# Row maxima of the second attention turned by VectorE in 32x32 blocks instead of by TensorE, and each unit's sums copied before a step's first exponential

## What is computed

```python
qkv = x @ w_qkv                      # x: layer norm of the tokens, (4, 1024, 256)
q, k, v = ...                        # 8 heads of 32 channels
dots = jnp.einsum('bhid,bhjd->bhij', q, k) * scale
attn = jax.nn.softmax(dots, axis=-1)
out = jnp.einsum('bhij,bhjd->bhid', attn, v)
t = t + out @ w_out + b_out
```

## Time and profile before

| | |
|---|---|
| time, median of 3 runs | 1183.61 us (1182.93 to 1188.93) |
| span of the profiled execution | 1183.2 us |
| busy, share of the span | PE 93%, PEld 62%, DVE 69%, ACT 53%, POOL 51% |
| mean granted TensorE clock | 0.985 of full |
| units whose row is turned in the second attention | 31 (one more is turned before it) |
| costliest groups beside PE's | L953 ACT 268.6 us, L1739 DVE 287.0 us, L699 POOL 197.8 us |

### The profile page before, as it was taken

The page is one execution under the profiler, slowest core; times in us unless marked ns, Lnnn a source line. Parts: engine busy times, 40 slices in busy tenths (PEclk is TensorE's granted clock), DMA queues, the critical chain, the costliest instruction groups (busy, mean ns, idle before and its releaser), DMA issues.

```text
span 1183.2 us, 28483 instructions
## 1 busy us (share of the span) xinstructions
PE 1105.0 (93%) x10344; PEld 728.7 (62%) x10344; DVE 818.8 (69%) x1493; ACT 628.7 (53%) x1144; POOL 600.2 (51%) x513
## 2 busy tenths in 40 slices
PE   7999999978999999999999989898999999999995
PEld 4454645434444454555445545687899988989883
DVE  4666566766788788788878892768555656655773
ACT  3566676546677666766775665453333333333332
POOL 3424242314888763775477546167545445544540
PEclk9999999989999999999999999999999999999999
DMA  5356842626123230433243213723333233323328
GB/s 173 89 181 211 311 160 94 184 69 196 51 56 87 82 82 29 104 100 98 68 115 91 60 43 100 303 38 77 53 54 54 43 52 55 46 46 47 46 38 289
DMA packets 98884, 120.60 MB, mean 102 GB/s; under 512 B 29024, under 2 KB 76064, under 8 KB 98112
## 3 DMA queue, kind: packets, MB, share of 16 engines
q1 hardware_dynamic: 75280, 70.40, 20.3%
q0 software_dynamic: 20400, 42.08, 15.9%
q10 hardware_dynamic: 3072, 6.30, 1.5%
HBM read 73.10 MB, written 45.47 MB: 100 GB/s over the span
## 4 chain that ended last, share of the span: by engine, by line
PE 70%; DVE 11%; issue 6%; DMA 6%; ACT 3%; DVEq 3%; POOL 1%; SPq 1%; ACTq 0%; POOLq 0%
PE PP L1023 21%; PE PP L1448 11%; PE PP L1307 9%; PE PP L1333 8%; PE PP L1122 3%; DVE mxp L1739 3%; PE PP L1254 3%; PE PP L1194 3%; PE PP L1039 3%; PE PP L1322 2%; PE PP L1317 2%; DMA res_d<-WORK,lb 2%; PE PP L1154 1%; DVEq L2016 1%; DVE WORK L2017 1%
## 5 line engine op out<-in xcount | busy, mean ns | idle before, releaser
L953 ACT ACTIVATE WB<-PP 128x512 f32<-128x512 f32 x512 | 268.6, 606 | 146.1 <-PE PP L1333 146.0
L1739 DVE TENSOR_REDUCE mxp<-PP 128x2 f32<-128x1024 f32 x242 | 287.0, 1219 | 62.3 <-PE PP L1254 62.0
L993 ACT ACTIVATE WORK<-PP,b1c 128x256 f32<-128x256 f32 (+1 forms) x320 | 139.4, 450 | 239.4 <-PE PP L1023 191.7
L699 POOL TENSOR_TENSOR WB<-WB 128x1024 f32<-128x1024 f32 x84 | 197.8, 2358 | 89.4 <-PE PP L1322 58.7
L782 POOL DMA_INDIRECT res_d<-WORK,lb x70 | 117.6, 1680 | 157.8 <-DVE WORK L2034 144.7
L1448 PE MATMUL PP<-WB,WORK 128*128 x1704 | 193.8, 274 | 0.0
L1023 PE MATMUL PP<-WORK,WB 128*128 128x256 f16 (+1 forms) x1552 | 175.9, 273 | 2.4 <-DVE WORK L2003 1.7
L1448 PEld LDWEIGHTS PP<-WB,WORK 128*128 128x128 f16 x1704 | 165.2, 98 | 19.6
L1023 PE MATMUL PP<-WORK 128*128 128x128 f16 (+6 forms) x1086 | 161.1, 300 | 11.3 <-DVE WORK L1656 3.6
L1023 PEld LDWEIGHTS PP<-WORK,WB 128*128 (+1 forms) x1552 | 152.2, 102 | 22.2 <-issue 4.8
L1333 PE MATMUL PP<-WORK 97*128 97x256 f16 x1024 | 158.0, 277 | 6.7 <-ACT WB L953 4.2
(11 more groups left out here) (319 smaller groups left out, 1205.1 us busy)
## 6 DMA issues: line engine op xcount, KB each, us to landing
WORK<-in_L_ffn_W_dram POOLq DMA_DIRECT2D x32, 512.0 KB, 4.3
res_d<-WORK SPq DMA_DIRECT2D x8, 1024.0 KB, 5.2
late_d<-WB POOLq DMA_DIRECT2D x1, 6144.0 KB, 19.3
WB<-late_d ACTq DMA_DIRECT2D x3, 2048.0 KB, 14.0
v_d<-WORK SPq DMA_DIRECT2D x4, 1024.0 KB, 5.2
WORK<-q_hi_d SPq DMA_DIRECT2D x16, 256.0 KB, 3.7
WORK<-v_d SPq DMA_DIRECT2D x8, 512.0 KB, 5.6
WORK<-k_hi_d SPq DMA_DIRECT2D x16, 256.0 KB, 3.9
```

The source lines that it names most:

```text
L699: pool.tensor_tensor(PS[n % 2], PR[n % 3][:, 0], PR[n % 3][:, 1], ALU.add).then_inc(s("pair_kept"), 1)
L953: act.activation(PR[n % 3][:, c // 2, c % 2 * 2:c % 2 * 2 + 2], SCORES[m % 3] .rearrange("p (h n) -> p h n", h=2), ACT.Exp).then_inc(s("e_ ...
L993: act.activation(hid[:, k, 0:width], hidden_bank(k)[:, 0:width], ACT.Gelu, bias=b1c[:, bass.ds(e, 1), k], scale=1.0 / WSCALE)\
L1739: dve.tensor_reduce(mxp[:, n // 4 % 2, i, h:h + 2, k], PP[2 + h // 2][:, :].rearrange("p (h n) -> p h n", h=2), X_AXIS, ALU.max).then_inc( ...
```

## The change

1. The row of maxima is turned by DVE. `turn_row` scales `mx` into a new SBUF tile `nm16` (128 x 2 x 32 in fp16, of which 2 x 4 are used), waits for that, and transposes 32x32 blocks into `nmr`, now 128 x 32 x 2. PE's transpose and DVE's copy out of PSUM are gone, and with them a slot in each unit.
2. A 32x32 transpose leaves 32 queries in a partition's row, so the row is stored with four DMAs of 4 x 64 values (one for each block of 32 partitions) instead of two of 4 x 128. For this the two query blocks of a unit are interleaved: the matmuls of maxima take every second query of 256 as weights (`max_queries`) instead of 128 in a row.
3. `keep_sums` stands ahead of a step's first exponential instead of behind it.
4. Of the last batch's tokens, the first unit's row is turned directly behind its joining, and PE's transpose and wait there are gone.

Line numbers in the diff's surroundings shift: `turn_row` is at L1614 to L1623 of the changed kernel.

```diff
@@ def group_place(n)
-    return unit // 4 % 2, unit % 4 * QN + i * P, k
+    return unit // 4 % 2, unit % 4 * QN, i, k
@@ buffers
-        nmr = sb("nmr", [2 * GH, P], F16)
+        nm16 = sb("nm16", [P, 2, D], F16)
+        nmr = sb("nmr", [P, D, 2], F16)
@@ SP: def store_max(b, u)
                 sp.wait_ge(s("nmr_kept"), b * UNITS + (u + 1))
                 par, at = u // 4 % 2, u % 4 * QN
-                for i in range(2):
-                    sp.dma_start(QP[QK_ROWS:QK_ROWS + 1, par, :, at + i * P:at + (i + 1) * P],
-                                 nmr[i * GH:(i + 1) * GH, :]).then_inc(s("ld_nm"), 16)
+                for q in range(P // D):
+                    sp.dma_start(QP[QK_ROWS:QK_ROWS + 1, par, :, at + 2 * D * q:at + 2 * D * (q + 1)],
+                                 nmr[q * D:q * D + GH, :, :]).then_inc(s("ld_nm"), 16)
@@ ACT: def attend(b)
                 for t in range(STEPS):
                     n = b * STEPS + t
+                    if t % 4 == 2 and n >= 6:
+                        keep_sums((n - 6) // 4)
                     if n >= 3:
                         act.wait_ge(s("pv_made"), FREE + n - 2)
                     for c in range(4):
...
-                        if c == 0 and t % 4 == 2 and n >= 6:
-                            keep_sums((n - 6) // 4)
@@ PE: maxima
+            def max_queries(rows_at, g, at, i):
+
+                return QM[rows_at, g, at + i:at + QN:2]
...
-                    mm = pe.matmul(PP[2 + h // 2][:, h % 2 * HALF:(h % 2 + 1) * HALF], QM[rows_at, g, at:at + P],
+                    mm = pe.matmul(PP[2 + h // 2][:, h % 2 * HALF:(h % 2 + 1) * HALF], max_queries(rows_at, g, at, i),
...
-            def max_row(b, u, before):
-
-                bank = next_slot(b, before)
-                pe.wait_ge(s("nm_kept"), b * UNITS + (u + 1))
-                pe.transpose(bank[0:2 * GH, 0:P], mx[:, :], identf[:, :]).then_inc(s("c_made"), 1)
@@ PE: def attend(b)
-                    u = row_unit(t, first, last)
-                    if u is not None:
-                        max_row(b, u, before)
@@ PE: tokens of the last batch
-                    pe.wait_ge(s("nm_kept"), 1)
...
-                    pe.transpose(PP[2][0:2 * GH, 0:P], mx[:, :], identf[:, :]).then_inc(s("c_made"), 1)
@@ DVE
+            def turn_row(b, u):
+
+                n = b * UNITS + u
+                dve.wait_ge(s("nm_kept"), n + 1)
+                dve.tensor_scalar(nm16[:, :, 0:GH], mx[:, :].rearrange("p (i h) -> p i h", i=2), 1.0 / MSCALE, None,
+                                  ALU.mult).then_inc(s("ns_kept"), 1)
+                dve.wait_ge(s("ns_kept"), n + 1)
+                if n:
+                    dve.wait_ge(s("ld_nm"), LOAD_ROW * n)
+                dve.transpose(nmr[:, :, :].rearrange("p c i -> p i c"), nm16[:, :, :]).then_inc(s("nmr_kept"), 1)
...
-            def keep_row(b, u, before):
-
-                bank = bank_made(before)
-                if b * UNITS + u > 0:
-                    dve.wait_ge(s("ld_nm"), 32 * (b * UNITS + u))
-                dve.tensor_scalar(nmr[:, :], bank[0:2 * GH, 0:P], 1.0 / MSCALE, None, ALU.mult)\
-                   .then_inc(s("c_kept"), 1)
...
                     u = row_unit(t, first, last)
                     if u is not None:
-                        keep_row(b, u, before)
-                        row_at = slots[0]
+                        turn_row(b, u)
```

More of the change, by code:

```diff
@@ L44 @@
 LOAD_MAX = 16 * 2
+LOAD_ROW = 16 * (P // D)
 QN = 256
@@ L75 @@
 NORM_PAIRS = {2: (0,), 3: (1, 2), 4: (3,)}
-BATCH_SLOTS = UNITS + NT + 1
-FIRST_SLOTS = 1 + UNITS
+BATCH_SLOTS = NT + 1
+COUNT_SLOTS = 1
 ROW = 2 * C
@@ L335, in slots_before @@
         def slots_before(b, first):
-            return FIRST_SLOTS - UNITS if first else b * BATCH_SLOTS + (FIRST_SLOTS - BATCH_SLOTS)
-        FINAL_SLOTS = FIRST_SLOTS + (B - 1) * BATCH_SLOTS
+            return 0 if first else (b - 1) * BATCH_SLOTS
+        FINAL_SLOTS = (B - 1) * BATCH_SLOTS + COUNT_SLOTS
         def slot_bank(before, k):
-            odd = before % 2 if isinstance(before, int) else FIRST_SLOTS % 2
-            return PP[2][:, (odd + k) % 2 * HALF:((odd + k) % 2 + 1) * HALF]
+            half = (before + k) % 2
+            return PP[2][:, half * HALF:(half + 1) * HALF]
         def hidden_bank(k):
@@ L1239, in next_slot @@
                 pe.wait_ge(s("mx_kept"), b * (2 * STEPS) + (2 * group[0] + 1))
-                if not isinstance(before, int) or before + at > others:
+                if before + at > others:
                     pe.wait_ge(s("c_kept"), before + (at - others))
@@ L1249, in max_group @@
                 pe.wait_ge(s("mx_kept"), b * (2 * STEPS) + 2 * n)
-                if not isinstance(before, int) or before + slots[0] > 0:
+                if before + slots[0] > 0:
                     pe.wait_ge(s("c_kept"), before + slots[0])
@@ L1524, in _ @@
             dve.memset(held16[:, :], 0.0)
+            dve.memset(nm16[:, :, :], 0.0)
             for i, dst in enumerate((wqT, wvT)):
@@ L1612, in keep_k, with join_halves @@
                                   kb.unsqueeze(1).broadcast_to((P, NT, P)), ALU.add).then_inc(s("k_kept"), 1)
+            def join_halves(u, b):
+                dve.wait_ge(s("mx_kept"), b * 2 * STEPS + 8 * (u + 1))
+                dve.tensor_reduce(mx[:, :], mxp[:, u % 2].rearrange("p i h k -> p (i h) k"), X_AXIS, ALU.max,
+                                  negate=True).then_inc(s("nm_kept"), 1)
+            def turn_row(b, u):
[7 more added lines that the diff above has]
+                dve.transpose(nmr[:, :, :].rearrange("p c i -> p i c"), nm16[:, :, :]).then_inc(s("nmr_kept"), 1)
             def early_max(j):
@@ L1650, in tokens @@
                     dve.drain()
-                    dve.tensor_reduce(mx[:, :], mxp[:, 0].rearrange("p i h k -> p (i h) k"), X_AXIS, ALU.max,
-                                      negate=True).then_inc(s("nm_kept"), 1)
+                    join_halves(0, 0)
+                    turn_row(0, 0)
                 dve.wait_ge(s("av_made"), b * NT + NT)
@@ L1673, in tokens @@
                 deviations("stat_kept")
-                if last:
-                    dve.wait_ge(s("c_made"), 1)
-                    dve.tensor_scalar(nmr[:, :], PP[2][0:2 * GH, 0:P], 1.0 / MSCALE, None, ALU.mult)\
-                       .then_inc(s("c_kept"), 1)
-                    dve.drain()
-                    dve.sem_inc(s("nmr_kept"), 1)
                 dve.wait_ge(s("sd_kept"), b + 1)
@@ L1740, in reduce_heads @@
                                   X_AXIS, ALU.max).then_inc(s("mx_kept"), 1)
-            def join_halves(u, b):
-                dve.wait_ge(s("mx_kept"), b * 2 * STEPS + 8 * (u + 1))
-                dve.tensor_reduce(mx[:, :], mxp[:, u % 2].rearrange("p i h k -> p (i h) k"), X_AXIS, ALU.max,
-                                  negate=True).then_inc(s("nm_kept"), 1)
-            def keep_row(b, u, before):
-                bank = bank_made(before)
-                if b * UNITS + u > 0:
-                    dve.wait_ge(s("ld_nm"), 32 * (b * UNITS + u))
-                dve.tensor_scalar(nmr[:, :], bank[0:2 * GH, 0:P], 1.0 / MSCALE, None, ALU.mult)\
-                   .then_inc(s("c_kept"), 1)
-            def row_kept(before, at):
-                dve.wait_ge(s("c_kept"), before + at)
-                dve.sem_inc(s("nmr_kept"), 1)
             logit, oh1, oh2, val, rest, tmp = [rt[:, i] for i in range(6)]
@@ L1941, in attend @@
                 slots[0] = 0
-                row_at = None
                 def tail_part(at):
@@ L1963, in attend @@
                     groups = max_groups(t, first, last)
-                    if row_at is not None:
-                        row_kept(before, row_at)
-                        row_at = None
                     joined = t + LEAD - 1
```

16 lines of the change are left out of this document (7 added, 9 removed).

## The result

| | before | changed |
|---|---|---|
| time, median | 1184.05 us (4 runs, 1182.93 to 1188.93) | 1204.18 us (4 runs, 1197.15 to 1210.04) |
| ratio to before, 95% interval | | 1.0158, 1.0107 to 1.0208 |
| span of the profiled execution | 1183.2 us | 1194.9 us (its own time: 1197.15 us, the lowest of the four) |
| mean granted TensorE clock | 0.985 | 0.981 |

The kernel became slower, by 20.1 us between the medians and by 18.7 us by the ratio. The prediction was 1201.2 us.

What follows compares the result with a forecast made beforehand. PE was taken to set the pace, with DVE free only about 0.55 us a step. The span of 1183.2 plus 23.3 for holds minus 5.7 of gains gave 1200.8, with 0.4 for the median 1201.2 us; range 1190 to 1211.

Steps and rivals of the forecast that it cites:

- The hold: DVE's new scaling between SBUF tiles (L1618) comes 0.4 us after POOL's addition L699 starts and stands until that ends.
- Its price: Delay per held unit: 1.49 us in the first batch (next maxima at 5.30 instead of 3.81), 1.0 us beside a projection.
- The count: Held: 7 first-batch units, t = 29 of second and third batch, t = 1, 5, 9 of three batches; 23.3 us.
- SP: SP's queue: four row DMA issues take about 2.5 us; row and sums just fit, by 0.3 us, and cost nothing.
- The gains: PE's transpose gone 3.3 us (30 by 0.11), copy ahead 1.9 (21 by 0.09), a slot less 0.5; together 5.7 us.
- Slow weights with a step of two: Rival: strided weight loads of the maxima cost 121 x 0.1 = 12 us on top of the hold: 1213; chance 0.03.
- Not held: Rival: the scaling L1618 isn't held by POOL, costs 0.2 us and fits the window: 1177.9 us; chance 0.12.
- nothing moves: Rival: holds cost half, POOL starting later relative to DVE, and the gains of 5.7 us cancel it: 1181 to 1187; chance 0.04.
- The margins give: Rival: row or sums land late, or the transpose is held or takes 0.55 us: about 1207 us; chance 0.08.

## Why the prediction was right, and where it was off

The time (1204.18 against 1201.2), the direction and the main mechanism held. Step by step:

- **The hold.** Right in place and kind. The scaling came 0.58 to 0.63 us into the step and stood until POOL's addition ended, 2.0 to 2.06 us. Shown by the reduction in its place (0.15 us, steps back to 2.90) and by the scaling added to the kernel before. The old scaling, which read PSUM, stood beside the same additions of POOL and was never held (source view, kernel before):

```profile
L1753 DVE TENSOR_SCALAR nmr<-PP x31: 267/269/279, 297.5 to 713.9; 8x128 f16<-8x128 f32 x31
```

- **Its price.** 1.31 us a unit in the first batch for 1.49. The group of maxima comes at 5.21 and not 5.30, mostly since the reductions start 0.08 us before the transpose's row ends; without a hold it would come at 3.85 and not 3.81, as the step before takes 3.09 and not 3.05; and PE wins 0.05 back behind it. Beside a projection 0.94 for 1.0.
- **The count.** 16 units, not 18. For t = 29 of the second and third batch I had read POOL's additions against a DVE that comes 0.6 us into the step. It comes 0.15 in, while POOL works at an L714 with an addition directly behind it. The timeline of DVE and POOL there, changed kernel:

```profile
514.62 1.15 POOL L714 TENSOR_TENSOR WORK<-WB,WORK 128x512 f16<-128x512 f32 x1
515.74 2.36 POOL L701 TENSOR_TENSOR WB<-WB 128x1024 f32<-128x1024 f32 x1
...
515.52 0.28 DVE L1618 TENSOR_SCALAR nm<-mx 128x8 f16<-128x8 f32 x1
```

  By these rows the scaling waits for the end of L714 only and gets in ahead of the addition. In the second profile of the same kernel it comes at 628.44, in the same place between L714 (to 628.86) and L701 (to 631.17), and stands through both:

```profile
628.44 2.77 DVE L1618 TENSOR_SCALAR nm<-mx 128x8 f16<-128x8 f32 x1
628.82 2.35 POOL L701 TENSOR_TENSOR WB<-WB 128x1024 f32<-128x1024 f32 x1
```

  So between two instructions of POOL it can go either way in the same kernel. Holds in all: 7.7 + 1.3 + 8.5 = 17.5 us in the first profile for 23.3.
- **SP.** Here the prediction failed. It said that two issues more and a held row cost nothing, and checked the row and the sums against their deadlines. Both indeed came in time. But behind them in the same queue stood the load of the next batch's values, which already came 1.14 us late before the change. Of the 3.42 us by which its issue moved in the first batch, 2.1 are the row, ready 2.95 us into its step (398.69) instead of 0.83 in, and 1.23 the two more issues. In the first profile it cost 7.7 - 1.3 = 6.4 us of waits and slow clock beyond before, in the second about 9 (11.7 without the 1.3 and without about 1.6 for the hold at t = 30 of the third batch); moving the load gave back 8.6 to 12.8 us, since the waits of before, 2.45 us, went with it.
- **The gains.** 0.11 us for the transpose was right in nearly every unit. The copy gave 0.05 to 0.06 instead of 0.09 as long as the transpose is gone, too, with weigh_heads 1.66 into the step and not 1.61 (397.40, the unit above), and nothing in the held units of the first batch, which the forecast had counted in. Together 5.0 us for 5.7 in the table's row; over the whole attention the copy's part is 0.8, by the run with the copy behind.
- **Not in the sum:** +2.4 us by the clock in the first steps, and -4.9 us in four steps. Of the latter, the kernel before had two holds of its own: L1873 and this one in the fourth batch,

```profile
703.12 1.84 DVE L1908 TENSOR_SCALAR WORK<-WORK 128x8 f32<-128x8 f32 x1
703.76 1.16 POOL L712 TENSOR_TENSOR WORK<-WB,WORK 128x512 f16<-128x512 f32 x1
...
706.14 0.40 PE L1254 MATMUL PP<-WB 32*128 32x512 f16 x4 [1.47 <-DVE mxp L1739]
```

  whose step took 6.30 us, half of it at low clock. It came 0.35 us into POOL's DMA instruction (702.77 to 703.73) and stood through this and the L712 behind it. After the change the same scaling, now L1893, comes 0.28 us into that DMA instruction (725.78 to 726.74) and isn't held, and the step takes 3.33:

```profile
726.06 0.17 DVE L1893 TENSOR_SCALAR WORK<-WORK 128x8 f32<-128x8 f32 x1
```

  Why the one was held and the other not stays open. Runs without the change to the row also had part of this gain (1.7 to 3.3 us), so it does not need the turned row; it is probably a matter of timing.
- **Rivals.** Slow weights with a step of two: the loads take 92 ns, before 91, so that rival is out. The Trainium skill, page "TensorE: Matmul & The Clock Gate", section "Weight-path perf modes — Fast Weight Load (FWL) and DoubleRow", calls such reads fast, packed or strided, and this agrees. "Not held" is out by the row of L1618, and "nothing moves" by the time, which lies above its 1187. "The margins give" came true in a form that I had not named: another transfer than the two that I had checked.

So 1201.2 came near 1204.18 partly by luck, because errors of opposite sign met: the holds were 5.8 us too dear, and 6.4 us of late values were missing; of the two terms that nobody had, one cost 2.4 us and the other gave 4.9. And the step table explains less than the medians differ by. Its profile is of the fastest of four executions, whose attention is 16.3 us longer than before but whose span is only 11.7 us longer, since the stretches around it were 4.6 us shorter together. What made the other three slower, up to 1210.04 us, is on no trace; the second profile (1200.12 us) had 4.1 us more of attention, by the late values and the hold described there.

What stays open: outside the second attention the profiles differ as well. The first stretch takes 289.0 to 290.7 us in the profiles with PE's transpose and 289.3 to 293.8 in those without; what comes behind the first scores of the last step takes 447.1 to 449.8 and 442.0 to 446.8. At least the first is in part a matter of the execution: the changed kernel itself took 292.5 and 289.6. Most kernels have one profile and no run was made on either stretch, so neither difference is explained.

## What to carry to other kernels

Before a scaling or a cast between SBUF tiles goes into VectorE's list, look at what GpSimd runs at that moment: a scaling of 0.16 us then lasted until GpSimd's instruction ended, up to 2.06 us, and a cast of 128x16 values (L1865, kernel before, at 459.26) took 1.73 us and ended 0.03 us behind POOL's addition. A reduction (0.15 us, if no factor is needed) or a source in PSUM (0.27 us) moved the same values without standing. When a wait or more issues are put into a queue, follow every transfer behind it to its next use, not only the ones that belong to the change, and issue those that wait for nothing ahead of the one that waits. Two savings in neighbouring engines may cover the same time; try each alone before adding them up.

## What the runs showed that I had not expected

- A stop of PE can cost twice. Behind the 3.01 us of waiting for the values PE worked 4.3 us at a granted clock of 0.60, 1.47 us more than the step needs at full clock. Behind the wait of 2.08 us at the end of the third batch the next step took its 2.90.
- A wait can go with a faster PE. Where it worked at half clock and in pieces, 0.80 us of waiting ahead of the pieces brought them together, and the three steps took 1.4 to 2.7 us less than without; but with the same work in one piece they once took 14.15 us instead of 12.74.
- Where two POOL instructions follow each other directly, a scaling that stands for the first sometimes gets in between (0.28 us) and once stood through both (2.77 us). In the kernel before with the scaling added it comes 0.14 us behind the start of the second and stands for that one alone (2.23 us).
